# A four-layer convolution network on one core: the first layer's software pipeline regrouped into other stages, and the last layer's silu one unit later

## The chip, the cores and the metric

The kernel runs on one core of one Trainium2 chip. The metric is the device time of one execution in microseconds; before and after are compared by the medians of several runs. Engines are named as in the profile: PE is TensorE, DVE VectorE, ACT ScalarE, POOL GpSimd, SP the engine that issues most DMAs.

## The reference, cut to what matters

The input x is 8 x 16 x 128 x 128 in float32. Each of four layers adds its result on x's group norm: `x = x + layer(_gn(x))`. The edits lie in the first and the last layer.

The first layer is a small transformer block for every pixel: three tokens (columns) of 48 features (16 channels times three rows, with wrap-around), normed, attention with four heads of 12 over the tokens, a residual, a norm, an MLP of 48 to 192 to 48 with Gelu, a residual, a norm, a sum over the tokens and a 1x1 convolution:

```python
h = _ln(x)
q, k, v = jnp.split(h @ w_attn.T, 3, axis=-1)
att = softmax(einsum('nhtd,nhsd->nhts', q, k) / sqrt(12))
x = x + (att @ v) @ w_attn_proj.T
x = x + gelu(_ln(x) @ w_fc.T) @ w_fc_proj.T
x = sum(_ln(x), axis=1)          # then conv_w, conv_b
```

The last layer is a 3x3 convolution of cubic B-spline bases of x plus a 3x3 convolution of silu(x).

## The kernel before, in words

**First layer** (`layer0`). The image is cut into 64 chunks (`NCHUNKS`): two images and eight columns at a time. A token column is 128 pixels. `steps` runs 67 rounds on each engine: three lead-in rounds, a loop of three rounds a pass (`TURNS`), and the last ones written out. In round n, four chunks are in work at different stages (`STAGE`): chunk n is "new", n-1 "attn", n-2 "mlp", n-3 "out". Each engine has its own order written out in its `body`; engines meet by counting semaphores alone, so an instruction that waits holds all behind it on that engine.

- new: `centre` (3 matmuls, TensorE) removes the mean; ScalarE reads it twice (`read_centre`: Square and Copy); `var1` sums the squares with a matmul of ones, `inverse_std` takes the reciprocal root on ScalarE, `scale_tokens` multiplies on GpSimd; `heads` (10 matmuls) makes query, key and value, `read_heads` copies them; `query_key` multiplies shifted queries and keys (three on VectorE, two on GpSimd), `score` reduces, `softmax_shift` subtracts the maximum.
- attn: Exp on ScalarE, `softmax_scale`, then `values` (9 multiplications, VectorE) and `add_values` (6 additions, GpSimd), `mix` (transposes), `read_mix`, `project`, and `add_attention` (VectorE), the first residual X1.
- mlp: `square_residual` (ScalarE), `var2`, `inverse_std`, `scale_residual` (VectorE); then for six groups g of 512 pixels `hidden` (two matmuls side by side), `hidden_rest`, three Gelus on ScalarE, `shrink` back, `add_mlp` (VectorE, X2); `square_out`.
- out: `var3`, `inverse_std`, `scale_out` and `add_out` on GpSimd, and the store.

PSUM has four pairs of banks, each used as a ring: tps (centre, var1, var2, var3, mix), qps (heads), fps (hidden), cps (shrink and project). `Plan` counts the places in the rings. Before a matmul goes into a bank, its reader of two places earlier must be done. TensorE's order in a round is `centre`, `var2`, `hidden(0)`, `var1`, `var3`, then groups of `hidden`, `shrink` of the group before, `hidden_rest`, two `heads` and one `mix`, and last `project`. VectorE's: `softmax_scale`, `values(0)`, `scale_residual`, `values(1)`, `values(2)`, `add_mlp` 0 to 4, the three products, `add_mlp(5)`, and `score` alternating with `add_attention`.

**Last layer** (`layer3`). 66 units n (a chunk k of four rows, in two halves e). In each unit ScalarE makes distances and squares, VectorE cubes and bases; after each two units TensorE multiplies chunk k's bases with the spline weights (`multiply(k)`) and then does `gather(k - 2)`, which takes the silu of chunks up to k-1 and the kept planes. The silu input S is loaded by GpSimd's own DMA queue (`load_silu`, three slots): load k waits for `gather(k - 3)` and for the load before. `silu_after(n)` says after which unit ScalarE does `silu(k)`: after units 3, 5, 7 and so on. `kept_after(n)` says which planes are copied out after a unit: two on ScalarE after odd units, one after even ones.

## Time and profile before

| | us |
|---|---|
| median of three runs | 11524.5 |
| those runs, lowest to highest | 11506.01 to 11528.91 |
| the profiled execution, its own time | 11512.45 |
| its span, first to last instruction | 11510.3 |
| busy in it: PE, DVE, ACT, POOL | 8808.3, 7862.0, 7497.3, 6400.2 |
| mean granted clock of TensorE, share of full speed | 0.877 |

Busy times are of one profiled execution. Busy shares mix four layers with different limits; the first layer's loop and the last layer's are read by themselves, from the stretches in which they run.

### The profile page before, as it was taken

Reading aid. Unit: us, or ns where it says so; the run is one execution under the profiler, and the core shown is the slowest. Engines: PE = TensorE matmul, PEld = TensorE weight load, DVE = VectorE, ACT = ScalarE, POOL = GpSimd, SP = SyncE. Lnnn points to the kernel's source line nnn. Section 1 sums busy time; section 2 is a strip of 40 time slices with the busy share of each in tenths; the row PEclk is TensorE's granted clock in tenths of the full one; section 3 lists DMA queues with packets and bytes.
Section 4 is the critical chain, followed back from the end, with each engine's and each line's share of the span. In section 5 each row is a group of like instructions: output and inputs, shape, how many; then the busy total and the mean of one; then the engine's idle time right before and its main releaser. Section 6 shows DMA issues by size and latency. Waiting matters only on the chain. (4 is left out here: it accounts for less than half of the span.)

```text
span 11510.3 us, 144669 instructions
## 1 busy us (share of the span) xinstructions
PE 8808.3 (77%) x35038; PEld 2895.7 (25%) x35038; DVE 7862.0 (68%) x9543; ACT 7497.3 (65%) x8343; POOL 6400.2 (56%) x3353
## 2 busy tenths in 40 slices
PE   5888888888888888844008888888888888885588
PEld 2333323333333333311002222222222222221133
DVE  5555565555556555643748888888888888886677
ACT  3555555555555555523419889889889988985577
POOL 3444444444444444420008888888888888885111
PEclk8888888888888888877559999999999999998799
DMA  2000000000000000010432322233223322234554
GB/s 74 9 9 7 8 9 9 7 9 9 9 7 9 9 7 9 4 62 29 141 106 60 67 62 59 60 68 65 60 60 67 67 60 60 65 66 91 138 126 117
DMA packets 284359, 562.90 MB, mean 49 GB/s; under 512 B 75120, under 2 KB 205904, under 8 KB 270172
## 3 DMA queue, kind: packets, MB, share of 16 engines
q1 hardware_dynamic: 247858, 536.71, 19.5%
q0 software_dynamic: 35744, 17.87, 0.8%
q8 instruction: 259, 4.24, 0.2%
q14 instruction: 498, 4.08, 0.1%
HBM read 367.98 MB, written 186.07 MB: 48 GB/s over the span
## 5 line engine op out<-in xcount | busy, mean ns | idle before, releaser
L1188 POOL TENSOR_TENSOR l_a<-l_a 128x1018 f32<-128x1018 f32 x2116 | 3920.9, 1883 | 600.4 <-ACT l_a L1349 587.4
L1311 DVE TENSOR_TENSOR l_r<-l_pps,l_a 128x509 f32<-128x509 f32 x4232 | 2642.3, 680 | 651.7 <-PE l_pps L1201 651.6
L1349 ACT ACTIVATE l_a<-l_a 128x2036 f32<-128x2036 f32 x1193 | 2270.1, 1903 | 126.4 <-DVE l_a L1317 100.5
L1201 PE MATMUL l_qps<-l_mv,l_wst 123*128 123x509 bf16 x4246 | 1318.7, 393 | 889.0 <-DMA l_mv<-pw 567.5
L1342 ACT ACTIVATE l_a<-l_qps 128x1018 f32<-128x1018 f32 x1592 | 1591.6, 1019 | 471.9 <-PE l_qps L1201 457.1
L586 POOL TENSOR_TENSOR a_pr<-a_pr 128x768 f32<-128x768 f32 x384 | 877.1, 2284 | 1248.2 <-DVE a_pr L529 1232.4
L540 DVE TENSOR_TENSOR a_x<-a_cps,a_x 128x512 f32<-128x512 f32 x384 | 260.8, 688 | 1624.2 <-PE a_cps L417 1142.8
L665 ACT ACTIVATE a_g<-a_fps 128x512 f32<-128x512 f32 x1152 | 646.0, 595 | 1110.7 <-PE a_fps L410 848.5
L1201 PE MATMUL l_pps<-l_mv,l_wst 123*128 123x509 bf16 x4232 | 1342.9, 389 | 10.9 <-DVE l_r L1311 5.0
L1254 PE MATMUL l_aux<-l_r,l_sums 128*32 128x509 f32 x8448 | 1129.4, 607 | 54.3 <-DVE l_o L1295 33.3
L463 POOL TENSOR_TENSOR a_pr<-a_qkv 128x768 f32<-128x768 f32 x128 | 344.3, 2707 | 1256.5 <-ACT a_qkv L671 1256.5
L1317 DVE TENSOR_SCALAR l_a<-l_qps 128x1018 int32<-128x1018 int32 x796 | 961.1, 1207 | 61.6 <-PE l_qps L1201 61.6
L644 ACT ACTIVATE a_r<-a_tps,a_eps 128x512 f32<-128x512 f32 (+1 forms) x960 | 638.5, 672 | 489.0 <-PE a_tps L370 230.4
L417 PE MATMUL a_cps<-a_g,a_wfp 128*64 128x512 f32 (+1 forms) x2304 | 904.8, 680 | 0.9 <-ACT a_g L665 0.9
L1201 PEld LDWEIGHTS l_qps<-l_mv,l_wst 123*128 123x128 bf16 x4246 | 300.5, 99 | 2031.7 <-issue 1107.5
L370 PE MATMUL a_tps<-a_h,a_ones 128*128 128x512 f32 x768 | 570.2, 902 | 307.6 <-ACT a_r L644 197.8
L529 DVE TENSOR_TENSOR a_pr<-a_qkv,a_at 128x768 f32<-128x768 f32 x576 | 792.7, 1437 | 2.2
L396 PE MATMUL a_cps<-a_yt,a_wproj 96*128 96x512 f32 x768 | 551.0, 866 | 252.7 <-DVE a_x L540 238.0
L410 PE MATMUL a_fps<-a_h,a_wfc 128*128 128x512 f32 x768 | 490.0, 723 | 171.7 <-ACT a_g L665 171.7
L1201 PEld LDWEIGHTS l_pps<-l_mv,l_wst 123*128 123x128 bf16 x4232 | 420.2, 99 | 766.0 <-DVE l_r L1311 358.8
L404 PE MATMUL a_fps<-a_h,a_wfc 48*128 48x512 f32 x1536 | 493.9, 723 | 61.6 <-ACT a_g L665 48.7
L533 DVE TENSOR_TENSOR a_h<-a_x,a_r 128x512 f32<-128x512 f32 x384 | 530.9, 1446 | 4.4 <-ACT a_r L644 4.4
(178 smaller groups left out, 11989.3 us busy)
## 6 DMA issues: line engine op xcount, KB each, us to landing
l_mv<-pw SPq DMA_DIRECT2D x1608, 79.5 KB
l_gx<-g SPq DMA_DIRECT2D x66, 1040.0 KB
planes<-l_s SPq DMA_DIRECT2D x67, 1018.0 KB, 4.6
l_sh<-planes SPq DMA_DIRECT2D x536, 127.2 KB, 6.5
a_xt<-g SPq DMA_DIRECT2D x192, 160.0 KB, 3.3
pw<-pw_hi SPq DMA_DIRECT2D x165, 127.2 KB
pw<-pw_mid SPq DMA_DIRECT2D x165, 127.2 KB
pw<-pw_lo SPq DMA_DIRECT2D x165, 127.2 KB
```

The source lines that it names most:

```text
L417: last = t_.matmul(cps[lo * FS:hi * FS, c % 2, :], flat(wfp[:, m, lo:hi, :]), G[:, g % 2, m, :], start=m == 1, stop=m == 2, skip_group_che ...
L529: v.tensor_tensor(out, val, a, ALU.mult).then_inc(val_v, 1)
L586: g_.tensor_tensor(y, y, PR[:, 3 * e + d, :], ALU.add).then_inc(val_p, 1)
L644: s_.activation(r, of, ACT.Abs_reciprocal_sqrt, bias=eps[:], scale=1.0 / EMB).then_inc(t_read, 1)
L665: s_.activation(G[:, g % 2, m, :], fps[:, bank % 2, :], ACT.Gelu).then_inc(f_read, 1)
L1188: g.tensor_tensor(a, a, a, ALU.mult).then_inc(sq_p, 1)
L1201: return t.matmul(out, wst[:, k, n * P:(n + 1) * P], x[:, n // NPP, cols], start=True, stop=True)
L1254: last = t.matmul(aux[32 * pp:32 * pp + 32, 0:SUB], sums[:, 0, :], R[:, NPP * k + pp, :], start=k == 0, stop=k == NCG - 1, skip_group_chec ...
L1311: v.tensor_tensor(to, pps[:, (2 * m + h) % P_BANKS, 0:SUB], pair_of(A, m)[:, h, :], ALU.mult).then_inc(mul_done, 1)
L1317: v.tensor_scalar(pair_of(A, s).bitcast(I32), q.bitcast(I32), 0x7FFFFFFF, None, ALU.bitwise_and).then_inc(abs_v, 1)
L1342: s_.activation(pair_of(A, s), q, ACT.Abs).then_inc(abs_a, 1)
L1349: s_.activation(a, a, ACT.Abs_reciprocal_sqrt, bias=1.0).then_inc(root_done, GROUP)
```

## The change

- First layer, stages: `centre`, `var1` and `scale_tokens` are a stage "ahead" (chunk n); `heads`, the products, the scores, the softmax shift and Exp are "new" (chunk n-1); attention with `square_residual`, `var2` and `scale_residual` is "attn" (n-2); the MLP with var3, `scale_out`, `add_out` and the store is "mlp" (n-3). There are still 67 rounds, and the loop has four to a pass. Tc has four slots in place of three, the input XT two in place of three, QKV two in place of one.
- The order in each engine's `body` is new, as the diff shows. Exp stands at the end of ScalarE's round. Two `mix` each stand in groups 3, 4 and 5.
- Last layer: `silu(k)` stands after unit 2k+4 in place of 2k+3.

Index changes that only follow from the new stage numbers are left out of the diff.

```diff
-TURNS = 3
+TURNS = 4
+SLOTS0 = 2
 BANK = 512
-T_GROUPS = {"centre": (3, "new"), "var2": (6, "mlp"), "var1": (3, "new"), "var3": (6, "out"), "mix": (6, "attn")}
+T_GROUPS = {"mix": (6, "attn"), "centre": (3, "ahead"), "var1": (3, "ahead"), "var3": (6, "mlp"), "var2": (6, "attn")}
 C_GROUPS = {"mlp": (6, "mlp"), "proj": (6, "attn")}
-STAGE = {"new": 0, "attn": 1, "mlp": 2, "out": 3}
+STAGE = {"ahead": 0, "new": 1, "attn": 2, "mlp": 3}
+MIX_AT = {3: (0, 1), 4: (2, 3), 5: (4, 5)}
...
-        self.new, self.attn, self.mlp, self.out = (0 <= like - of < NCHUNKS for of in STAGE.values())
+        self.ahead, self.new, self.attn, self.mlp = (0 <= like - of < NCHUNKS for of in STAGE.values())
...
-        XT = sb("a_xt", [F2, TURNS, TW * H])
+        XT = sb("a_xt", [F2, SLOTS0, TW * H])
...
-        QKV = sb("a_qkv", [P, TW, 3 * F2])
+        QKV = sb("a_qkv", [P, 2, TW, 3 * F2])
...
-                    if n + TURNS < NCHUNKS:
+                    if n + SLOTS0 < NCHUNKS:
                         sp.wait_ge(t_made, p.t_base + p.t_at["centre"] + 3)
-                        load(n + TURNS)
-                    if p.out:
+                        load(n + SLOTS0)
+                    if p.mlp:
...
                 def heads(p, w):
                     if w == 0:
-                        pe.wait_ge(h1_made, p.n * 3 + 3)
-                    pe.wait_ge(q_read, p.n * TW + w + 1)
+                        pe.wait_ge(h1_made, p.n * 3)
+                    pe.wait_ge(q_read, (p.n - 1) * TW + w + 1)
                     t_.matmul(qps[:, w % 2, 0:3 * F2], H1[:, w * H:(w + 1) * H], wqkv[:], start=True, stop=True).then_inc(q_made, 1)
                 def mix(p, q):
                     if q % 2 == 0:
-                        pe.wait_ge(val_p, (p.n - 1) * 6 + q + 2)
+                        pe.wait_ge(val_p, (p.n - 2) * 6 + q + 2)
...
                 def body(p):
-                    if p.new:
-                        pe.wait_ge(x_in[p.turn], (p.n - p.turn) * 16 + 48)
-                        for g in range(3):
-                            centre(p, g)
-                    if p.mlp:
-                        for g in range(6):
-                            var2(p, g)
-                        hidden(p, 0)
-                    if p.new:
-                        for g in range(3):
-                            var1(p, g)
-                    if p.out:
-                        for g in range(6):
-                            var3(p, g)
                     for g in range(7):
-                        if p.mlp and 0 < g < 6:
+                        if p.mlp and g < 6:
                             hidden(p, g)
                         if p.mlp and g:
                             shrink(p, g - 1)
                         if p.mlp and g < 6:
                             hidden_rest(p, g)
-                        if p.new and 0 < g < 6:
-                            heads(p, 2 * g - 2)
-                            heads(p, 2 * g - 1)
-                        if p.attn and g:
-                            mix(p, g - 1)
+                        if p.new and g < 5:
+                            heads(p, 2 * g)
+                            heads(p, 2 * g + 1)
+                        if p.attn:
+                            for q in MIX_AT.get(g, ()):
+                                mix(p, q)
+                    if p.ahead:
+                        pe.wait_ge(x_in[p.turn % SLOTS0], (p.n - p.turn % SLOTS0) * 24 + 48)
+                    for g in range(6):
+                        if p.attn:
+                            project(p, g)
+                        if p.ahead:
+                            (centre if g < 3 else var1)(p, g % 3)
+                    if p.mlp:
+                        for g in range(6):
+                            var3(p, g)
                     if p.attn:
                         for g in range(6):
-                            project(p, g)
+                            var2(p, g)
...
-                def products(p):
-                    dve.wait_ge(q_read, p.n * TW + TW + 2)
-                    if p.attn:
-                        dve.wait_ge(val_p, p.n * 6)
-                    for d in (-1, 0, 1):
-                        query_key(v, d).then_inc(sc_v, 1)
+                def products(p, d):
+                    if d == -1:
+                        dve.wait_ge(q_read, p.n * TW + 2)
+                        if p.attn:
+                            dve.wait_ge(val_p, (p.n - 1) * 6)
+                    query_key(v, p, d).then_inc(sc_v, 1)
...
-                    if g == 0 and p.out:
+                    if g == 0:
...
                 def body(p):
                     if p.attn:
                         softmax_scale(p)
                         values(p, 0)
                     if p.mlp:
+                        add_mlp(p, 0)
+                    if p.attn:
+                        values(p, 1)
+                    if p.mlp:
+                        add_mlp(p, 1)
+                    if p.attn:
+                        values(p, 2)
+                    if p.mlp:
+                        for g in range(2, 6):
+                            add_mlp(p, g)
+                    for g in range(6):
+                        if p.attn:
+                            add_attention(p, g)
+                        if p.new and g in (1, 2, 3):
+                            products(p, g - 2)
+                    if p.new:
+                        for n in range(5):
+                            score(p, n)
+                        softmax_shift(p)
+                    if p.attn:
                         for g in range(6):
                             scale_residual(p, g)
-                    if p.attn:
-                        values(p, 1)
-                        values(p, 2)
-                    if p.mlp:
-                        for g in range(5):
-                            add_mlp(p, g)
-                    if p.new:
-                        products(p)
-                    if p.mlp:
-                        add_mlp(p, 5)
-                    for g in range(6):
-                        if p.new and g < 5:
-                            score(p, g)
-                        if p.attn:
-                            add_attention(p, g)
-                    if p.new:
-                        softmax_shift(p)
...
+                pool.sem_inc(z_made, 3)
...
                 def body(p):
                     if p.attn:
-                        add_values(p, 0)
+                        for d in range(3):
+                            add_values(p, d)
                     if p.new:
+                        pool.wait_ge(q_read, p.n * TW + 2)
+                        if p.attn:
+                            pool.wait_ge(val_p, (p.n - 1) * 6)
+                        for d in (-2, 2):
+                            query_key(g_, p, d).then_inc(sc_p, 1)
+                    if p.ahead:
                         for g in range(3):
                             scale_tokens(p, g)
-                    if p.attn:
-                        add_values(p, 1)
-                        add_values(p, 2)
-                    if p.out:
+                    if p.mlp:
                         for d in range(3):
                             scale_out(p, d)
-                    if p.new:
-                        pool.wait_ge(q_read, p.n * TW + TW + 2)
-                        if p.attn:
-                            pool.wait_ge(val_p, p.n * 6)
-                        for d in (-2, 2):
-                            query_key(g_, d).then_inc(sc_p, 1)
-                    if p.out:
                         add_out(p)
...
-                    if w == 0 and p.attn:
-                        act.wait_ge(val_v, p.n * 9)
-                    act.wait_ge(q_made, p.n * TW + w + 1)
-                    s_.activation(QKV[:, w, :], qps[:, w % 2, 0:3 * F2], ACT.Copy).then_inc(q_read, 1)
+                    act.wait_ge(q_made, (p.n - 1) * TW + w + 1)
+                    s_.activation(QKV[:, (p.turn - 1) % 2, w, :], qps[:, w % 2, 0:3 * F2], ACT.Copy).then_inc(q_read, 1)
...
                 def body(p):
-                    if p.new:
+                    for g in range(6):
+                        if p.mlp:
+                            gelu(p, g)
+                        if p.new and g < 5:
+                            read_heads(p, 2 * g)
+                            read_heads(p, 2 * g + 1)
+                        if p.attn:
+                            for q in MIX_AT.get(g, ()):
+                                read_mix(p, q)
+                        if p.mlp and g in (3, 5):
+                            square_out(p, g // 4)
+                    if p.ahead:
                         for g in range(3):
                             read_centre(p, g)
                     if p.mlp:
-                        for d in range(3):
-                            square_residual(p, d)
+                        square_out(p, 2)
+                    if p.ahead:
+                        for g, (w, n) in enumerate(CENTRE):
+                            inverse_std(p, "var1", g, R1[:, w * H:(w + n) * H])
+                    if p.mlp:
+                        act.wait_ge(stored, (p.n - 3) * (SETS * 16) + 16)
+                    for g in range(6):
+                        if p.attn and g % 2 == 0:
+                            square_residual(p, g // 2)
+                        if p.mlp:
+                            inverse_std(p, "var3", g, R3[:, g // 2, g % 2 * BANK:(g % 2 + 1) * BANK])
                     if p.attn:
-                        act.wait_ge(soft, (p.n - 1) * 9 + 6)
-                        s_.activation(At[:], At[:], ACT.Exp, scale=float(HEAD) ** -0.5).then_inc(soft_exp, 1)
-                    if p.mlp:
                         for g in range(6):
                             inverse_std(p, "var2", g, R2[:, g, :])
                     if p.new:
-                        for g, (w, n) in enumerate(CENTRE):
-                            inverse_std(p, "var1", g, R1[:, w * H:(w + n) * H])
-                    if p.out:
-                        act.wait_ge(stored, (p.n - 3) * (SETS * 16) + 16)
-                        for g in range(6):
-                            inverse_std(p, "var3", g, R3[:, g // 2, g % 2 * BANK:(g % 2 + 1) * BANK])
-                    for g in range(7):
-                        if p.mlp and g < 6:
-                            gelu(p, g)
-                        if p.new and 0 < g < 6:
-                            read_heads(p, 2 * g - 2)
-                            read_heads(p, 2 * g - 1)
-                        if p.attn and g:
-                            read_mix(p, g - 1)
-                    if p.mlp:
-                        for d in range(3):
-                            square_out(p, d)
+                        act.wait_ge(soft, (p.n - 1) * 9 + 6)
+                        s_.activation(At[:], At[:], ACT.Exp, scale=float(HEAD) ** -0.5).then_inc(soft_exp, 1)
...
             def silu_after(n):
-                return (n - 3) // PARITY if n >= 3 and n % PARITY else None
+                return (n - 4) // PARITY if n >= 4 and n % PARITY == 0 else None
```

## Rows read from the trace of the kernel before

**Rows 1.** Windows: stretch, us, busy of each engine (instructions), PEclk, DMA share, GB/s.

```profile
77.00:5063.00 4986.00, 4118.92 (x10496) 1516.03 (x10496) 2831.36 (x2816) 2570.60 (x4163) 2298.66 (x1024) 0.85 0.04 8
...
10756.00:11508.00 752.00, 649.26 (x3664) 232.80 (x3660) 552.78 (x321) 569.04 (x387) 132.71 (x190) 0.92 0.51 122
```

**Rows 2.** Timeline of TensorE, first layer: start, us, line, passes, idle before.

```profile
2504.20 2.13 PE L417 MATMUL a_cps<-a_g,a_wfp 128*128 128x512 f32 x6
...
2507.22 1.13 PE L381 MATMUL a_qps<-a_wqkv,a_h 128*128 128x288 f32 x4
2508.19 0.60 PE L389 MATMUL a_tps<-a_ident,a_pr 128*96 128x128 f32 x4
...
2509.78 2.14 PE L417 MATMUL a_cps<-a_g,a_wfp 128*128 128x512 f32 x6
...
2532.69 7.56 PE L396 MATMUL a_cps<-a_yt,a_wproj 96*128 96x512 f32 x10 [3.83 <-DVE a_x L540]
...
2569.43 2.06 PE L410 MATMUL a_fps<-a_h,a_wfc 128*128 128x512 f32 x2 [2.69 <-ACT a_g L665]
...
4983.86 1.13 PE L404 MATMUL a_fps<-a_h,a_wfc 48*128 48x512 f32 x4 [0.34 <-ACT a_g L665]
```

**Rows 3.** Windows of one round, cut at its changes of clock.

```profile
2531.83:2538.65 6.82, 5.96 (x7) 2.37 (x8) 6.82 (x10) 1.06 (x1) 4.77 (x2) 0.51 0.12 22
...
2545.48:2555.72 10.24, 7.26 (x9) 2.42 (x8) 7.01 (x7) 6.99 (x9) 2.18 (x1) 0.51 0.08 15
...
sum 77.37, PE 64.12 PEld 23.76 DVE 45.09 ACT 40.91 POOL 37.20; mean PE 9.16 PEld 3.39 DVE 6.44 ACT 5.84 POOL 5.31
```

**Rows 4.** Timeline of TensorE: `hidden(0)` of the first and last chunk, var3.

```profile
166.26 1.13 PE L404 MATMUL a_fps<-a_h,a_wfc 48*128 48x512 f32 x4 [0.75 <-DVE a_h L533]
...
5004.86 1.13 PE L404 MATMUL a_fps<-a_h,a_wfc 48*128 48x512 f32 x4
5005.92 5.85 PE L375 MATMUL a_tps<-a_sq,a_ones 128*128 128x512 f32 x12
```

**Rows 5.** Timeline of ScalarE, same round: around Exp, one Gelu.

```profile
2546.60 1.28 ACT L685 ACT_TABLE_LOAD   x1
2547.89 0.68 ACT L685 ACTIVATE a_at<-a_at 128x576 f32<-128x576 f32 x1
...
2571.52 0.60 ACT L665 ACTIVATE a_g<-a_fps 128x512 f32<-128x512 f32 x1 [1.66 <-PE a_fps L410]
```

**Rows 6.** Timeline of VectorE: values alone, then beside GpSimd's adds.

```profile
2551.63 2.69 DVE L529 TENSOR_TENSOR a_pr<-a_qkv,a_at 128x768 f32<-128x768 f32 x3
...
2562.16 10.11 DVE L529 TENSOR_TENSOR a_pr<-a_qkv,a_at 128x768 f32<-128x768 f32 x6
```

**Rows 7.** DMA issues of the page: KB each, median us to landing.

```profile
l_gx<-g SPq DMA_DIRECT2D x66, 1040.0 KB
...
a_xt<-g SPq DMA_DIRECT2D x192, 160.0 KB, 3.3
```

**Rows 8.** ScalarE's groups, 5250 to 10550 us: busy, mean ns, idle before.

```profile
L1349 ACT ACT_TABLE_LOAD x1 | 1.3, 1283 | 0.0
```

**Rows 9.** Groups of instructions, 10600 to 11511 us: the silu activations.

```profile
L1604 ACT ACTIVATE l_s<-l_s 128x1040 f32<-128x1040 f32 x33 | 35.3, 1070 | 149.4 <-DMA l_s<-g 149.4
```

**Rows 10.** ScalarE's silu(0) and silu(1), TensorE's gather(0), in order of time.

```profile
10773.73 1.07 ACT L1604 ACTIVATE l_s<-l_s 128x1040 f32<-128x1040 f32 x1
...
10791.60 1.07 ACT L1604 ACTIVATE l_s<-l_s 128x1040 f32<-128x1040 f32 x1
...
10804.29 5.33 PE L1718 MATMUL l_ops<-l_s,l_wba 128*64 128x512 f32 x36
```

**Rows 11.** GpSimd's DMA queue in order of time: a wait for the load before.

```profile
10945.63 0.66 POOL L1579 DMA_DIRECT2D l_s<-g  x1 [31.49 <-DMA l_s<-g]
```

**Rows 12.** Windows of two stretches in the last layer.

```profile
11163.00:11200.00 37.00, 37.00 (x222) 13.16 (x220) 33.44 (x20) 34.53 (x24) 8.13 (x12) 1.00 0.59 157
10924.00:10975.00 51.00, 41.17 (x236) 14.67 (x234) 33.36 (x20) 34.65 (x24) 8.52 (x12) 0.90 0.51 111
```

More of the change, by code:

```diff
@@ L166, in ring @@
         for name, (size, of) in groups.items():
-            if {"new": self.new, "attn": self.attn, "mlp": self.mlp, "out": self.out}[of]:
+            if {"ahead": self.ahead, "new": self.new, "attn": self.attn, "mlp": self.mlp}[of]:
                 at[name], k = k, k + size
@@ L283, in layer0 @@
         w_in, cw_made, cw_ready, cent_made, w_ready = (sem(f"a_{n}") for n in ("w_in", "cw_made", "cw_ready", "cent_made", "w_ready"))
-        x_in = [sem(f"a_x_in{k}") for k in range(TURNS)]
+        x_in = [sem(f"a_x_in{k}") for k in range(SLOTS0)]
         stored = sem("a_stored")
@@ L303, in load @@
                     for i in range(3):
-                        sp.dma_start(XT[i * SETS * C:(i + 1) * SETS * C, n % TURNS, :].rearrange("p (w h) -> p w h", h=H),
-                                     rows[:, w0:w0 + TW, i:i + H]).then_inc(x_in[n % TURNS], 16)
-                for n in range(TURNS):
+                        sp.dma_start(XT[i * SETS * C:(i + 1) * SETS * C, n % SLOTS0, :].rearrange("p (w h) -> p w h", h=H),
+                                     rows[:, w0:w0 + TW, i:i + H]).then_inc(x_in[n % SLOTS0], 16)
+                for n in range(SLOTS0):
                     load(n)
@@ L357, in centre @@
                     w, n = CENTRE[g]
-                    t_.matmul(place(p, "centre", g)[:, 0:n * H], flat(wcen[:]), XT[:, p.turn, w * H:(w + n) * H],
+                    t_.matmul(place(p, "centre", g)[:, 0:n * H], flat(wcen[:]), XT[:, p.turn % SLOTS0, w * H:(w + n) * H],
                               start=True, stop=True).then_inc(t_made, 1)
@@ L504, in softmax_shift @@
                 def softmax_shift(p):
-                    b = p.n * 9
-                    dve.wait_ge(sc_v, p.n * 8 + 8)
+                    b = (p.n - 1) * 9
+                    dve.wait_ge(sc_v, p.n * 8)
                     top = sm[:, 0, :].rearrange("p (d n) -> p d n", d=3)
@@ L545, in add_attention @@
                     dve.wait_ge(c_made, p.c_base + c + 1)
-                    v.tensor_tensor(X1[:, g, :], cps[:, c % 2, :], Tc[:, (p.turn - 1) % TURNS, at:at + BANK], ALU.add).then_inc(c_read, 1)
+                    v.tensor_tensor(X1[:, g, :], cps[:, c % 2, :], Tc[:, (p.turn - 2) % TURNS, at:at + BANK], ALU.add).then_inc(c_read, 1)
                 def body(p):
```

35 lines of the change are left out of this document (17 added, 18 removed).

## The prediction

> **What bounds the kernel.** I read the stages first. The first layer's loop takes 4986 us with TensorE busy 4119 of them, the last layer's loop 752 us [rows 1]; the edits touch nothing else, and the 5.7 ms between stay as they are.
>
> In the first layer I then read one round on TensorE in order of time [rows 2]. In the MLP groups the matmuls stand back to back: group to group 5.58 us, of which two `heads` 0.97. Outside them TensorE stands still: 3.83 us before `project(1)` (`add_mlp(5)` was queued behind the three products on VectorE), 2.69 us before `hidden_rest(0)` (ScalarE had var3's roots and a table load first), and others, smaller. The stages of that round show 64.12 us busy of 77.37, so 13.2 us idle, and three stretches at the granted clock 0.51, that is mostly 1.2 GHz: twice 6.8 us (the first is shown) and once 10.2; each follows such a hole [rows 3], and at 1.00 (2.4 GHz) the same work runs without loss. VectorE is busy 45, ScalarE 41, GpSimd 37 us of a round: none of them is the bound as a sum.
>
> The work of TensorE in a round at 2.4 GHz: six groups, less one pair of `heads`, 6 x 5.58 - 0.97 = 32.5; `var3`, `var2`, `project`, 12 passes of 512 columns each, 5.85 apiece [rows 4] = 17.5; `centre` and `var1`, five passes' worth each of 0.486 = 4.9. Sum 54.9. So 77.4 = 54.9 + 13.2 idle + 9.3 lost to the clock. The first chunk's `hidden` starts at 166.3 and the last one's at 5004.9 [rows 4]: 63 rounds apart, of which 61 have all four stages (rounds 3 to 63, a matter of the code).
>
> **First layer, part by part.** No arithmetic, matmul or DMA is added or removed; `centre`/`norm` of a chunk, its `heads` and products, its attention and its MLP now stand in four successive rounds, and var3 in the MLP's own. I walk the new queues from S, the end of `shrink(5)`, at full clock.
>
> TensorE has `project(g)` alternating with `centre`/`var1`, so the wait for `add_attention(g-2)` falls under the other matmul. The products stand behind `add_attention(1)`, with GpSimd's two products long done, and the only add ahead of `project(1)` is `add_mlp(5)` (0.6). Ends at S+10.7, its 10.7 of work. If the products ran at the values' shared rate, 1.69 us for 768 columns [rows 6] and so 1.9 each, `project(5)` would be some 2 us late; I take half the chance of it in the range.
>
> ScalarE is next: centre reads to S+6.1, `square_out(2)` 1.0, table load 1.3, `var1` roots to 11.2, then three squares of 1.0 among the six `var3` roots. TensorE runs two matmuls ahead of it in two banks, so `var3` and `var2` end at S+23.4 in place of 22.3: 1.1 lost. The last root ends at 24.2. Then the queue asks for a table load, Exp, a table load and Gelu: 1.28 + 0.68 + 1.28 and 0.60 [rows 5], so `hidden_rest(0)` starts at 28.2, while `hidden(0)` ended at 24.5: a hole of 3.7. The softmax shift, done at S+18.4, is no longer what Exp waits for. `scale_residual(0)` starts at 19.3, so `hidden` does not wait for it.
>
> After that 31.5 us of MLP groups: the groups without mixes have only `heads` (0.97) to cover the Gelu between `hidden_rest` and the next `hidden`; in the old tail a group with a mix alone (0.53) stood 0.34 short [rows 2], so 0.87 is enough. VectorE: scale of the softmax to 30.5 (3.0), `values(0)` to 33.1, `values(1)` and `values(2)` at the shared rate of 10.1 us for six [rows 6], to 42 and 47; `add_mlp(1)` at 42 is needed by `shrink(3)` at 47.3, the sums for `mix(0)` (39.4) at 45.5, those for `mix(4)` (49.5) at 56.7. Nothing waits: slack of 5 us and more. The x loads have two buffers in place of three, but a load of 3.3 us [rows 7] is asked for a full round ahead; the store is awaited half a round later. Both cost nothing; without that cover each would show as a wait before `centre` or before the first `var3` root.
>
> Full clock round: 54.9 + 1.1 + 3.7 = 59.7. One hole of 3.7 us is left, like the one of 3.83 after which the clock was low for 6.8 us; I charge one such stretch a round, 6.8 at half speed less what falls in the hole: 2.9. **Round 62.6.** Full rounds save 61 x (77.37 - 62.6) = 901. Fill and drain: chunk 0's Exp no longer stands before chunk 1's `var1` (first MLP at about 150, not 166), and the last MLP has no var3 of another chunk inside (5): with the lighter rounds 64 and 65, 28. Together 929.
>
> Does an interleaved Square or Copy reload a table? In layer 2 Abs, root, Square and Copy ran a whole layer on one load [rows 8]; so nothing.
>
> On `values` beside `add_values`, the row says 1.69 us each in place of 0.87. The Trainium skill, SBUF — State Buffer, "Who interferes with whom", says that a VectorE instruction with two SBUF inputs and a GpSimd one that reads SBUF block each other for whole instructions. By it every value could wait for a whole add, 2.3 us by the page of the profile, and take 3.2: `add_mlp(1)` would be 4.5 later, still inside the 5 of slack, the sum unchanged but the second last rival below nearer.
>
> **Last layer.** `silu(k)` moves one unit later in ScalarE's queue, 8.9 us (silu(0) to silu(1), two units, 17.9 [rows 10]). Its waits for the POOL queue's S load sum to 149.4 us [rows 9]. Behind it stand Squares, on which VectorE's bases and so TensorE depend. Its user, `gather(k-1)`, starts 11.7 us after it (silu(1) ends 10792.7, gather(0) starts 10804.3) [rows 10], so 2 us of slack remain and the move itself costs nothing. If loads came as they do, each wait would shrink by up to 8.9: 105 of the 149. But the POOL queue waited up to 31.5 us for a load to land [rows 11], beside gx loads of 1040 KB a unit [rows 7], and when ScalarE no longer stops, gx loads no longer pause. A stretch without stalls moved 157 GB/s with TensorE always busy, one with them 111 [rows 12]: the room is there at times only. Bounds 0 and 105; I take 45, nearer the zero since the load's own length stays. The Trainium skill, SBUF — State Buffer, "SBUF: two separate sides", says that descriptors for a DMA of the GpSimd queue can't be written while VectorE is in a two-port operation. By that the loads lengthen as VectorE's pauses vanish, and this part would be worth 0.
>
> **Sum.** 11512.5 (the profiled execution; span 11510.3 and 2.1 around it) - 929 - 45 = 10538, say 10540. The runs shown have a median of 11524.5, 12 more; a tenth of a per cent, left aside. No change can be told within 0.2%, some 23 us.
>
> **Rivals.**
> - Forecast, a round of 61 to 65 us: 0.60. With the last layer's bounds 10,380 to 10,730.
> - The clock never falls in the 3.7 us hole: round 59.7, 61 x 2.9 = 177 less: 10,360. The holes of 2.69 and 3.83 speak against. 0.10.
> - The clock stays low longer, or falls again between var3's roots where TensorE waits 0.3 to 0.5 each time; before it once stayed for 10.2 us [rows 3]. 3.4 us more a round: 10,750. With late products, 10,870. 0.19.
> - ScalarE reloads tables after all, six loads of 1.28 in the stretch it sets: 7.7 a round, 11,010. The single load of [rows 8] speaks against. 0.04.
> - The other side: the values under the MLP hold `add_mlp(1)`, `shrink(3)` waits, and the six values before it decide. From 5 us late each microsecond costs one a round; from 20 us late, when they take 4.5 us each and not 1.3, the change is slower. At 5.5 each: 25 late, round 82.7, 11,512 + 61 x 5.3 - 45 = 11,790. Nothing in [rows 6] shows such rates. 0.03.
> - The old bound was not TensorE's queue but something I have not seen, and the round stays near 77: 11,470 to 11,530. Against: the gaps close exactly where the trace names them. 0.04, half of it within 0.2%.
>
> **Numbers.** The range takes the first three, with some of the clock's bad side: 10,350 to 10,850 leaves out under 0.2. Faster: all but the last two, with half of the last lying below: 0.95; same 0.02, slower 0.03.
>
> **What would show it.** Right: rounds of 61 to 65 us, four to a loop pass, TensorE busy some 58 of them; one hole of 3 to 4 us before `hidden_rest(0)` put down to Gelu, no hole before `project(1)`; one stretch of low clock a round and the mean clock of the layer above 0.93; no wait of `mix` for GpSimd; Silu's waits below 105 us and no new wait of `gather` over 4 us. Wrong: a wait of `shrink` for `add_mlp`, more than three table loads a round, two low stretches, or silu waits of the same sum as before.

## The result, and the profile after

| us | before | after |
|---|---|---|
| median | 11518.51 (4 runs) | 10461.89 (4 runs) |
| lowest to highest | 11506.01 to 11528.91 | 10454.87 to 10472.31 |
| span of the profiled execution | 11510.3 | 10453.1 |
| mean granted clock | 0.877 | 0.912 |

The ratio is 0.9084, 95% interval 0.9068 to 0.9100: 1057 us less, where 10540 with a range of 10350 to 10850 was predicted. The windows of the two stages of the kernel after correspond to [rows 1]:

```profile
77.00:4060.00 3983.00, 3662.69 (x10494) 1439.99 (x10492) 2709.98 (x2816) 2516.70 (x4162) 2046.02 (x1024) 0.94 0.05 11
9755.00:10451.00 696.00, 612.69 (x3624) 223.22 (x3620) 544.07 (x316) 556.29 (x382) 122.28 (x184) 0.94 0.54 130
```

The same work now fills 92% of the first layer's loop (83% before) at a granted clock of 0.94 (0.85 before). The first layer can be accounted for by TensorE's `hidden(0)`; those of its first and last chunk correspond to [rows 4], and between them stands the one of chunk 61, with which the last full round ends:

```profile
149.83 1.13 PE L406 MATMUL a_fps<-a_h,a_wfc 48*128 48x512 f32 x4 [0.38 <-DVE a_h L531]
...
3897.74 1.69 PE L406 MATMUL a_fps<-a_h,a_wfc 48*128 48x512 f32 x4 [3.09 <-DVE a_h L531]
...
4008.98 1.13 PE L406 MATMUL a_fps<-a_h,a_wfc 48*128 48x512 f32 x4
```

In the kernel before, chunk 61's is this one:

```profile
4877.89 1.13 PE L404 MATMUL a_fps<-a_h,a_wfc 48*128 48x512 f32 x4
```

The 63 rounds from the first to the last took 4838.60 us before and 3859.15 now, 979.4 less. The 61 full rounds among them took 4711.6 before and 3747.9 now, that is 77.24 and 61.44 each, 963.7 less; the two lighter ones behind them give 15.7. The first `hidden(0)` is 16.4 earlier. The layer's end, read at the next layer's first DMA, went from 5064.15 to 4061.46, so it follows the last `hidden(0)` by 52.5 in place of 59.3: 6.8 more. Together 1002.7. The spans differ by 1057.2, which leaves 54.5 for everything behind the first layer, the silu's move in it.

One round of TensorE in order of time corresponds to [rows 2]; S, the end of `shrink(5)` of the round before, is at 2520.36, and the next S at 2583.28:

```profile
2520.36 1.13 PE L398 MATMUL a_cps<-a_yt,a_wproj 96*128 96x512 f32 x2
2521.32 1.02 PE L360 MATMUL a_tps<-a_xt,a_wcen 96*128 96x512 f32 x2
...
2529.92 1.94 PE L377 MATMUL a_tps<-a_sq,a_ones 128*128 128x512 f32 x4
2532.26 4.08 PE L377 MATMUL a_tps<-a_sq,a_ones 128*128 128x512 f32 x8 [0.40 <-ACT a_r L643]
2536.64 5.97 PE L372 MATMUL a_tps<-a_h,a_ones 128*128 128x512 f32 x12 [0.29 <-ACT a_r L643]
2545.43 1.13 PE L406 MATMUL a_fps<-a_h,a_wfc 48*128 48x512 f32 x4 [2.82 <-DVE a_h L531]
2547.29 2.08 PE L412 MATMUL a_fps<-a_h,a_wfc 128*128 128x512 f32 x2 [0.73 <-ACT a_g L664]
...
2553.23 3.81 PE L419 MATMUL a_cps<-a_g,a_wfp 128*128 128x512 f32 x6
```

The idle times are 0.40, 0.29, 2.82 and 0.73: 4.2 of 62.9. The holes of 3.83 and 2.69 are gone; what is left is one pair of holes around `hidden(0)`, the larger one not before `hidden_rest(0)` but before `hidden(0)` itself, put down to VectorE's `scale_residual`. Windows cut around it, and one at the same place of the round before, show the clock: it is the number behind the five busy times.

```profile
2485.10:2491.90 6.80, 6.13 (x12) 2.36 (x10) 6.70 (x10) 2.77 (x6) 0.03 (x1) 0.50 0.02 4
...
2520.36:2545.43 25.07, 21.39 (x50) 8.35 (x49) 22.35 (x23) 19.39 (x29) 15.00 (x8) 1.00 0.09 21
...
2547.80:2555.50 7.70, 7.70 (x14) 2.62 (x14) 6.02 (x7) 2.50 (x5) 2.37 (x1) 0.50 0.00 0
2555.50:2581.60 26.10, 26.10 (x95) 10.75 (x94) 9.63 (x11) 13.69 (x28) 14.03 (x8) 0.98 0.00 1
```

One stretch at 0.50 (1.2 GHz) follows the hole. In the round shown it is 10.2 us long (2546.5 to 2556.8), in the round before 6.8, and 6.8 is the rule: of the 61 full rounds six take 62.9 us or more, like the one shown, most others 61.3. That is the forecast stretch. Why `hidden(0)` waits is in VectorE's rows, and why nothing could have started earlier anyway in ScalarE's, which correspond to [rows 5]. VectorE:

```profile
2535.51 2.16 DVE L510 TENSOR_TENSOR a_at<-a_sc,a_sm 128x192 f32<-128x192 f32 x1
2537.70 0.37 DVE L509 TENSOR_REDUCE a_sm<-a_sc 128x64 f32<-128x192 f32 x1
2538.11 1.99 DVE L510 TENSOR_TENSOR a_at<-a_sc,a_sm 128x192 f32<-128x192 f32 x1
...
2542.68 2.60 DVE L531 TENSOR_TENSOR a_h<-a_x,a_r 128x512 f32<-128x512 f32 x1 [0.15 <-DVE a_at L510]
```

GpSimd at the same time, and then ScalarE:

```profile
2532.77 7.12 POOL L598 TENSOR_TENSOR a_r<-a_x,a_r 128x1024 f32<-128x1024 f32 x3 [0.51 <-ACT a_r L643]
```

```profile
2543.35 1.28 ACT L705 ACT_TABLE_LOAD   x1
2544.65 0.68 ACT L705 ACTIVATE a_at<-a_at 128x576 f32<-128x576 f32 x1
2545.35 1.28 ACT L664 ACT_TABLE_LOAD   x1
2546.64 1.08 ACT L664 ACTIVATE a_g<-a_fps 128x512 f32<-128x512 f32 x2
```

A subtraction of 192 elements a partition takes 2 us while GpSimd multiplies beside it (the third one, 2.00, runs beside GpSimd's addition of `add_out`); the reductions between, which read one tile, keep their 0.37. The shift therefore ends at S+22.2, not S+18.4, and `scale_residual(0)` starts 3 us late. Then it takes 2.60 us itself, beside GpSimd's second addition of 2.34, where the six of the round together take 5.61. ScalarE is not free for Gelu before 2546.64 in any case.

In the last layer the group of silus (the second row) corresponds to [rows 9]; the first row is `gather`'s silu part, which waits for it:

```profile
L1717 PE MATMUL l_ops<-l_s,l_wba 128*64 128x256 f32 (+1 forms) x1152 | 188.7, 483 | 68.9 <-ACT l_s L1603 68.9
...
L1603 ACT ACTIVATE l_s<-l_s 128x1040 f32<-128x1040 f32 x33 | 35.1, 1064 | 97.5 <-DMA l_s<-g 97.4
```

Silu's waits fell from 149.4 to 97.5 us, and `gather`'s waits for silu rose from 17.8 to 68.9, up to 11.5 at once. TensorE's wait for the bases went from 121.1 to 88.4 and that for the kept planes from 37.9 to 0.

### The profile page after: what moved, and what is told of

Its sections match the earlier page's. It is cut to its first block and busy times, and to the rows that moved or that the text cites. A ratio compares the mean times of both kernels' runs of the same rounds, so it can differ in the third digit from the quotient of the medians.

```text
span 10453.1 us, 144566 instructions
## 1 busy us (share of the span) xinstructions
PE 8327.9 (80%) x35038; PEld 2814.5 (27%) x35038; DVE 7741.3 (74%) x9543; ACT 7442.2 (71%) x8342; POOL 6142.6 (59%) x3353
## 5 line engine op out<-in xcount | busy, mean ns | idle before, releaser
L588 POOL TENSOR_TENSOR a_pr<-a_pr 128x768 f32<-128x768 f32 x384 | 854.0, 2224 | 739.3 <-DVE a_pr L527 723.4
L419 PE MATMUL a_cps<-a_g,a_wfp 128*64 128x512 f32 (+1 forms) x2304 | 832.1, 635 | 0.7 <-ACT a_g L664 0.7
L527 DVE TENSOR_TENSOR a_pr<-a_qkv,a_at 128x768 f32<-128x768 f32 x576 | 714.9, 1294 | 2.2
L594 POOL TENSOR_TENSOR a_h<-a_tc,a_r 128x512 f32<-128x512 f32 (+1 forms) x192 | 205.2, 1097 | 845.0 <-ACT a_r L643 845.0
L598 POOL TENSOR_TENSOR a_r<-a_x,a_r 128x1024 f32<-128x1024 f32 x192 | 454.7, 2399 | 98.4 <-ACT a_r L643 98.4
L1578 POOL DMA_DIRECT2D l_s<-g x66 | 44.6, 676 | 687.0 <-DMA l_s<-g 388.3
L383 PE MATMUL a_qps<-a_wqkv,a_h 128*128 128x288 f32 x1280 | 429.3, 465 | 9.6 <-POOL a_h L594 6.8
```

Source lines behind the costliest of these rows:

```text
L419: last = t_.matmul(cps[lo * FS:hi * FS, c % 2, :], flat(wfp[:, m, lo:hi, :]), G[:, g % 2, m, :], start=m == 1, stop=m == 2, skip_group_che ...
L527: v.tensor_tensor(out, val, a, ALU.mult).then_inc(val_v, 1)
L588: g_.tensor_tensor(y, y, PR[:, 3 * e + d, :], ALU.add).then_inc(val_p, 1)
```

## Experiments

Each kernel differs from the one after the change by the edit shown, unless it says otherwise; ratios are to the kernel before, with 95% intervals.

### The two parts by themselves

The first kernel is the one after with the old `silu_after`; the second is the one before with the new `silu_after`:

```diff
-                return (n - 4) // PARITY if n >= 4 and n % PARITY == 0 else None
+                return (n - 3) // PARITY if n >= 3 and n % PARITY else None
```

> The changed kernel with the last layer's silu put back after unit 2k+3. My theory (the two parts add up, the silu's part is worth about 50 us): 10,510 us, silu waits back near 149 us. Rival (the last layer is bound by its DMA traffic and the silu's place is worth nothing, the 54 us were shift between layers): 10,462 within 15 us.

Measured: 10511.41, ratio 0.9121 (0.9105 to 0.9136). Silu waited 159.4 us.

> The kernel before with the silu alone moved to unit 2k+4. Additive: 11,465 us, ratio 0.9955, and in the trace the waits move in part from ScalarE's Silu to TensorE's gather, sum of Silu waits near 98 us. Rival (DMA bound): ratio 1.000 within 0.002.

Measured: 11481.12, ratio 0.9962 (0.9946 to 0.9978). Silu waited 102.9 us, `gather` for it 72.8.

The silu's move is worth 36 us alone and 50 on top of the first layer's change (43 by the two ratios): the parts add up within the intervals. The first layer's change alone gives 1006, near the 1002.7 of its account above.

### Is it the alternation, or only the stages?

```diff
-                    for g in range(6):
-                        if p.attn:
+                    if p.attn:
+                        for g in range(6):
                             project(p, g)
-                        if p.ahead:
-                            (centre if g < 3 else var1)(p, g % 3)
+                    if p.ahead:
+                        for g in range(3):
+                            centre(p, g)
+                        for g in range(3):
+                            var1(p, g)
```

> The changed kernel with the six project matmuls first, then the centre and var1 ones, instead of one of each in turn. In the trace of the changed kernel a 512-column matmul in turn took 0.86 us, and 0.97 where a matmul follows one of the same bank ring. My theory: 0.97 is the round trip of two banks (matmul, its reader, the next matmul), so without the turns the stretch grows by 11 x 0.11 = 1.2 us plus waits for the products between the adds, 2 to 4 us a round, 10,590 to 10,700. Rival (0.86 comes from something else, such as the size of the operands): start to start stays 0.86 and the time grows only by the products' waits, under 60 us.

Measured: 10673.0, ratio 0.9263 (0.9248 to 0.9279), 211 us above the kernel after, 3.5 a round. TensorE's timeline shows where they go:

```profile
2537.03 1.12 PE L398 MATMUL a_cps<-a_yt,a_wproj 96*128 96x512 f32 x2 [0.44 <-DVE a_x L547]
2538.69 1.12 PE L398 MATMUL a_cps<-a_yt,a_wproj 96*128 96x512 f32 x2 [0.54 <-DVE a_x L547]
2541.85 0.70 PE L360 MATMUL a_tps<-a_xt,a_wcen 96*128 96x256 f32 x2 [0.32 <-ACT a_tc L652]
2542.93 1.98 PE L367 MATMUL a_tps<-a_sq,a_ones 128*128 128x512 f32 x4 [0.38 <-ACT a_tc L652]
2546.42 0.69 PE L367 MATMUL a_tps<-a_sq,a_ones 128*128 128x256 f32 x2 [1.51 <-ACT a_r L646]
2546.99 1.98 PE L377 MATMUL a_tps<-a_sq,a_ones 128*128 128x512 f32 x4
```

These are the waits for the reader of a bank, with no other matmul under them. From S (2532.69 here) to the first `var3` matmul it is 14.3 us, where the kernel after needs 9.6: 4.7 more. That the round grows by 3.5 only goes with the clock, whose mean over 500 to 3800 us is 0.97 here and 0.94 in the kernel after. And the four undisturbed `project` matmuls of this kernel start every 0.95 to 0.96 us (3.90 for the four, as 5.85 for six in [rows 4]), where those of the kernel after start every 0.86. The next kernel asks which of the two is the matmul's own time: on top of the edit above, `project(2)` and `project(3)` go into the heads' banks, and `add_attention` reads them there, so that a bank's reader has longer.

```diff
-                    pe.wait_ge(c_read, p.c_base + c + 1)
-                    t_.matmul(cps[:, c % 2, :], flat(wproj[:]), yT[:, g, :], start=True, stop=True).then_inc(c_made, 1)
+                    if g in (2, 3):
+                        pe.wait_ge(q_read, min(p.n, NCHUNKS) * TW + 2 if isinstance(p.n, int) else p.n * TW + 2)
+                        to = qps[:, g % 2, :]
+                    elif g >= 4:
+                        pe.wait_ge(c_read, p.c_base + c - 1)
+                        to = cps[:, c % 2, :]
...
+                    t_.matmul(to, flat(wproj[:]), yT[:, g, :], start=True, stop=True).then_inc(c_made, 1)
```

> Like the run without the turns, but project(2) and project(3) write the two banks that the heads use, so no project waits for the add two before it until project(4). Round-trip theory: start to start of the projects falls to 0.86 at least for the first four. Rival (matmuls with the same weights one after the other take 0.97 whatever the bank): 0.97 stays.

Measured: 10624.58, ratio 0.9227 (0.9212 to 0.9243), 48 less than with two banks. Pairs of `project`, TensorE's timeline:

```profile
2564.77 1.88 PE L406 MATMUL a_qps<-a_yt,a_wproj 96*128 96x512 f32 x4
2566.49 1.88 PE L406 MATMUL a_cps<-a_yt,a_wproj 96*128 96x512 f32 x4
2568.21 1.88 PE L360 MATMUL a_tps<-a_xt,a_wcen 96*128 96x512 f32 x4
...
2575.55 1.98 PE L377 MATMUL a_tps<-a_sq,a_ones 128*128 128x512 f32 x4
```

1.72 from pair to pair, 0.86 a matmul: the 0.97 that I had read as a matmul's duration is the round trip of a ring of two banks, that is matmul, reader, next matmul into the same bank. From S (2562.95) to `var3` it is now 12.6 us, 1.7 less than with two banks, and the round 0.8 less, at a mean clock of 0.95. The waits of `centre` and `var1` stayed (0.32, 0.38, 1.51), so more banks for `project` alone don't replace the alternation.

### What is behind the hole that is left

The rows suggest two chains that end together: VectorE's and ScalarE's. The first kernel shortens ScalarE's chain by one table load: Square stands in for Exp, so the attention weights are other numbers.

```diff
-                        s_.activation(At[:], At[:], ACT.Exp, scale=float(HEAD) ** -0.5).then_inc(soft_exp, 1)
+                        s_.activation(At[:], At[:], ACT.Square, scale=float(HEAD) ** -0.5).then_inc(soft_exp, 1)
```

> The changed kernel with Square in place of Exp in the softmax (the attention weights are then others, all else is computed as before), so that ScalarE has one table load less, 1.28 us, between the last root and the first Gelu. My theory: two chains end together at hidden_rest(0), ScalarE's (Exp and its loads) and VectorE's (the shift's three subtractions, 2.0 us each beside GpSimd's multiplications and not 0.36, then scale_residual(0), for which hidden(0) waits 2.8 us). Then this gains at most 0.1 us a round: 10,455 to 10,470. Rival (ScalarE's chain alone sets it, as predicted): 1.28 x 63 = 80 us less, 10,380.

Measured: 10470.94, ratio 0.9093 (0.9079 to 0.9107): no gain. `hidden(0)` waits 2.80 for `scale_residual` as before. The second kernel takes GpSimd's multiplications, and the additions behind them, away from the shift:

```diff
                     if p.mlp:
+                        if p.new:
+                            pool.wait_ge(soft, (p.n - 1) * 9 + 6)
                         for d in range(3):
                             scale_out(p, d)
```

> The changed kernel with GpSimd's scale_out held until the softmax shift of the round is done. The shift's subtractions should take 0.36 us each again, and hidden(0) should no longer wait for scale_residual(0). My theory of two chains that end together: the time stays, 10,440 to 10,480, since ScalarE's chain still sets the first Gelu, and the hole moves to hidden_rest(0). Rival (the block on VectorE alone costs the hole): 2.8 x 63 = 176 us less, 10,290.

Measured: 10459.74, ratio 0.9080 (0.9067 to 0.9092): no gain either, but the rows move. VectorE's shift, then TensorE:

```profile
2537.95 0.36 DVE L510 TENSOR_TENSOR a_at<-a_sc,a_sm 128x192 f32<-128x192 f32 x1
2538.34 0.37 DVE L509 TENSOR_REDUCE a_sm<-a_sc 128x64 f32<-128x192 f32 x1
2538.75 0.36 DVE L510 TENSOR_TENSOR a_at<-a_sc,a_sm 128x192 f32<-128x192 f32 x1
```

```profile
2544.98 1.13 PE L406 MATMUL a_fps<-a_h,a_wfc 48*128 48x512 f32 x4
2549.73 1.12 PE L412 MATMUL a_fps<-a_h,a_wfc 128*128 128x512 f32 x2 [3.62 <-ACT a_g L666]
```

That is the round the prediction had walked: no wait of `hidden(0)`, one hole of 3.6 before `hidden_rest(0)`. The subtraction takes 0.36 us alone and 2.0 beside GpSimd's multiplications. Now both edits in one kernel:

> The after kernel with Square in place of Exp (the attention weights are other numbers) and GpSimd's scale_out held until the softmax shift is done. Each of the two alone left the time as it was. Theory (two chains end within half a microsecond of each other before hidden(0) and hidden_rest(0): VectorE's shift and scale_residual, ScalarE's two table loads and Gelu): with both shortened the hole shrinks by the one table load, 1.28 us a round, 61 x 1.28 = 78 us: about 10,380, with one hole of 2.3 us before hidden_rest(0). If that shorter hole no longer brings the granted clock down, another 61 x 2 us: about 10,260. Rival (a third thing sets the hole, neither chain): 10,460 again.

Measured: 10304.96, ratio 0.8952 (0.8931 to 0.8973): 157 us less than the kernel after, where neither edit alone moved anything. It is more than the 78 of the table load, and less than with a clock that never falls; over 500 to 3800 us the mean clock is 0.97, with either edit alone 0.94. Windows that begin at the end of the hole (at 2503.7 after one of 2.96, at the others after one of 2.20) show the clock:

```profile
2503.70:2512.00 8.30, 7.59 (x15) 3.02 (x16) 8.27 (x6) 4.08 (x7) 5.34 (x2) 0.59 0.11 20
2565.40:2573.00 7.60, 7.57 (x18) 3.14 (x19) 7.57 (x6) 2.97 (x6) 5.10 (x2) 0.79 0.10 17
2623.90:2632.00 8.10, 8.03 (x26) 3.21 (x26) 8.06 (x6) 4.21 (x10) 5.15 (x2) 1.00 0.10 16
```

After the holes of 2.20 the granted clock stays at 1.00 in one round and falls for a part of the stretch in others; the hole of 2.96 comes once in four rounds and is put down to no other engine:

```profile
PE a_fps L412 <- ACT a_g L666: 105.5, 57, 2.2
PE a_fps L406 <- issue: 37.9, 13, 3.3
```

From 500 to 3800 us there are thirteen such waits, 2.9 each, always before the first matmul of a loop pass of four rounds: that is the place of the way back to the loop's start. In the kernel after, the hole before `hidden(0)` is as long as they are, so they don't show there and come out when it closes.

### What the clock itself costs

Four matmuls whose result nobody reads stand before `hidden(0)`, in the bank that it overwrites:

```diff
                 def body(p):
+                    if p.mlp:
+                        pe.wait_ge(f_read, (p.n - 3) * 18 + 2)
+                        for _ in range(FILL):
+                            t_.matmul(fps[:, 0, 0:3 * P], ones[:], wfp[:].rearrange("p m s f -> p (m s f)"), start=True, stop=True)
                     for g in range(7):
```

> The changed kernel with four extra matmuls of 384 columns on constant weights, about 0.64 us each, into the hidden banks in the hole before hidden(0); their results are overwritten. Theory (the low clock after the hole is what it costs, 2.9 us a round): granted clock of the layer near 1.00 and 10,290 to 10,350. Rival (the clock falls anyway, or the extra work comes late and pushes hidden(0)): 10,460 to 10,520.

Measured: 10316.84, ratio 0.8956 (0.8943 to 0.8968), 145 us less than the kernel after, with no wait taken away but the filled one. From 500 to 3800 us the granted clock is 1.00 with the extra work, 0.94 without. Two extra matmuls in place of four, and four with the GpSimd edit from above:

> Two extra matmuls before hidden(0) in place of four: 1.95 us of the 2.8 us hole before hidden(0) is filled, 0.9 us stays open, and the 0.7 us before hidden_rest(0) too. Theory A (any hole under some 2 us is ridden out: the holes of 0.3 to 0.7 us that the round has elsewhere did not bring the clock down): granted clock near 1.00, 10,310 to 10,330. Theory B (it takes a nearly closed hole): the clock falls in part of the rounds, mean 0.94 to 0.98 in the first layer, 10,360 to 10,460.

> Four extra matmuls before hidden(0), as in the kernel with the filled hole (10,317 us), and GpSimd's scale_out held until the softmax shift is done. Theory (the gain of the filled hole is the clock's alone): hidden(0) never waits for scale_residual, the extra matmuls end 0.2 us later than ScalarE's chain needs, the clock stays at 1.00 and the time is that of the filled hole, 10,300 to 10,330. Rival: with both chains off VectorE's shift, hidden_rest(0) starts up to 0.5 us earlier a round: 10,290. A result above 10,400 would say that what was left of the hole lay behind the extra matmuls and brings the clock down again.

Measured: two matmuls 10332.25, ratio 0.8980 (0.8965 to 0.8995); four with GpSimd behind the shift 10322.03, ratio 0.8969 (0.8954 to 0.8984). The two-matmul kernel still has a hole before `hidden(0)`, on TensorE's timeline:

```profile
2581.98 1.13 PE L407 MATMUL a_fps<-a_h,a_wfc 48*128 48x512 f32 x4 [1.53 <-DVE a_h L536]
2583.85 1.13 PE L413 MATMUL a_fps<-a_h,a_wfc 128*128 128x512 f32 x2 [0.74 <-ACT a_g L669]
```

and its granted clock is 0.99 over 500 to 3800 us. The first window below begins at that `hidden(0)`. The other two begin at the extra matmuls behind the hole at the loop's start, in two passes that follow each other: the hole was 3.05 us in the one and 3.09 in the other.

```profile
2581.00:2592.00 11.00, 9.28 (x30) 3.52 (x30) 10.90 (x14) 6.94 (x13) 2.59 (x2) 1.00 0.07 12
2517.97:2526.00 8.03, 7.35 (x12) 2.92 (x13) 7.93 (x11) 2.67 (x4) 0.57 (x1) 0.50 0.08 16
...
2282.73:2291.00 8.27, 7.59 (x24) 2.83 (x24) 8.10 (x11) 4.76 (x8) 0.86 (x1) 1.00 0.08 15
```

After 3.05 the granted clock is 0.50, after 3.09 it stays at 1.00. From 500 to 3800 us, windows of some 8 us show it at 1.00 after 38 of this kernel's 43 holes of about 1.5 us before `hidden(0)`, and below (0.57 to 0.79) after the other five. It stays at 1.00 after four of this kernel's thirteen holes at the loop's start (2.5 to 3.1 us), and after eight of the thirteen (2.5 to 3.05) in the kernel with four extra matmuls; after the others it falls for all or a part of the stretch. So in these two kernels the length of the hole alone does not decide it.

What the extra matmuls bring back is the clock's part, 130 to 145 us; the two chains behind the hole stay, and moving GpSimd adds nothing that the intervals show. The three filled kernels can't be told apart by their intervals; each beats both the kernel before and the one after. The 10304.96 of the kernel with both shortened chains does not stand beside them, since Square is not the reference's Exp.

### The last layer: who paces silu

One more unit of delay:

```diff
-                return (n - 4) // PARITY if n >= 4 and n % PARITY == 0 else None
+                return (n - 5) // PARITY if n >= 5 and n % PARITY else None
```

> The after kernel with silu(k) after unit 2k+5 in place of 2k+4 in the last layer. Theory (after the first move gather already waits for silu 69 us in all, up to 9.5 at once, so what ScalarE no longer waits TensorE does): silu's own waits fall from 97 to 40 to 60 us, gather's rise by more than as much, to 150 us or over, and the time is 0 to 60 us longer: 10,460 to 10,520. Rival (ScalarE's waits are what the layer pays, TensorE has 83 us idle in it to give): another 20 to 45 us less, 10,415 to 10,440.

Measured: 10474.5, ratio 0.9096 (0.9081 to 0.9112), not told from the kernel after. Its two groups:

```profile
L1717 PE MATMUL l_ops<-l_s,l_wba 128*64 128x256 f32 (+1 forms) x1152 | 195.0, 495 | 87.3 <-ACT l_s L1603 87.3
...
L1603 ACT ACTIVATE l_s<-l_s 128x1040 f32<-128x1040 f32 x33 | 35.2, 1068 | 100.0 <-DMA l_s<-g 99.9
```

The time lies in the range of the theory, and the rival's further gain did not come; but silu's waits did not fall to 40 to 60 us, and `gather`'s rose to 87 and not to 150. The waits of silu for its load and of `gather` for silu together were 167 us before, 166 after and 187 here: the first move shifted them to an engine that had them to give, the second adds to `gather`'s alone. A reading that fits, and that no run isolates: the load of S waits for `gather(k - 3)` in its turn and comes later with it (GpSimd's queue waited 116.8 us for `gather` after the change, up to 25.8 at once, and 123.4 here, up to 41.9). Then the load itself, from GpSimd's queue to SP's (`load_silu` moves with its calls):

```diff
+                    if n == 2:
+                        for i in range(PSLOTS):
+                            load_silu(i)
+                    elif n % PARITY and (n - 5) // PARITY >= PSLOTS:
+                        load_silu((n - 5) // PARITY)
                     if n >= GX:
                         sp.wait_ge(v_done, n - GX + 1)
...
-                for k in range(NCK):
-                    load_silu(k)
```

> The changed kernel with the last layer's S loads on SP's queue, among the gx loads, in place of GpSimd's. Rival A (the loads are late because GpSimd writes their descriptors beside VectorE): loads land in some 15 us, silu and gather waits go, 10,350 to 10,400. Rival B (the DMA traffic sets it: S and gx loads share the engines): the waits stay or move to the gx loads, 10,440 to 10,520. I hold B the likelier.

Measured: 10685.44, ratio 0.9271 (0.9257 to 0.9285), 224 us slower than the kernel after. Its waits:

```profile
ACT l_vb L1598 <- DMA l_gx<-g: 394.0, 31, 50.9
...
PE l_ops L1719 <- ACT l_s L1605: 211.3, 28, 9.1
```

Silu waits 4.9 us for its load now, but ScalarE waits 394 for gx, 66 before this edit: the waits of the S loads stand ahead of the gx loads in one queue (SP waits 247.8 us there for the S load before). The waits moved to the gx loads, as rival B has it, but by the order of one queue, which tells nothing of shared DMA engines, and the time is 165 us above its range. So this kernel doesn't tell what makes a load of GpSimd's queue late, and neither expectation is borne out.

## Why the prediction was right, by its own steps

- **The sum.** 929 + 45 = 974 forecast, 1057 measured. The first layer gave 1002.7 (74 more), the rest 54.5 (9 more).
- **Round 62.6.** The full rounds take 61.44 on average, where 77.24 was their average before (77.37 was one round), and save 963.7 where 901 was forecast, 63 more; a fill and drain 11 larger than forecast (below) makes it 74. The forecast had S to `hidden_rest(0)` 28.2 and from there 31.5 + 2.9; the rows show 26.9, and in the round before the one shown, with its low stretch of 6.8 us, 34.3 (2486.07 to 2520.36). The kernel with four extra matmuls, whose clock stays up, needs 31.5 for the same work (2524.72 to 2556.19). So the MLP's part and the clock's 2.9 are both right to 0.1.
- **The mis-sized term: 5.85 for 12 passes of `project`, 10.7 us for it with `centre` and `var1`.** It took 9.6. The 0.97 a matmul of [rows 4] holds the round trip of two banks; where another ring's matmul lies between, it is 0.86, and the four-bank kernel shows the same without alternation. This is the term that made the round shorter than forecast. ScalarE's last root ends at S+23.0, not 24.2, and everything behind it is earlier by that.
- **Softmax shift done at S+18.4, `hidden(0)` not waiting.** Wrong: S+22.2, and `hidden(0)` waits 2.8. I had weighed the Trainium skill's rule in SBUF — State Buffer, "Who interferes with whom", for the values and not for the small subtractions; there the trace agrees with it, 0.36 alone and 2.0 beside GpSimd. It cost nothing, since ScalarE's table loads end at the same time: removing either alone gives 0, both 157. That the time did not suffer from this step is luck: the prediction counted on ScalarE's chain alone. It is why `hidden(0)`, and not `hidden_rest(0)`, has the larger hole.
- **One hole of 3.7, after it a clock stretch of 2.9.** Right in size: 2.82 + 0.73, and filling it gives 145 us, 2.4 a round of 61; the once-in-four hole at the loop's start stays in that kernel.
- **No reload by interleaved Square or Copy.** Right: three loads a round, one each before var1's roots, Exp and Gelu; none at the squares or copies between the roots.
- **Values under the MLP cost nothing.** Right: neither `mix` nor `shrink` has a wait among the layer's. The six were priced at 10.1 us; they take 2.68 and 3.66, since GpSimd's adds run between them for the most part.
- **Fill and drain, 28.** Of the measured 1002.7 the full rounds leave 39: the first `hidden(0)` 16.4 earlier, as forecast, the two lighter rounds 15.7 and the end 6.8.
- **Silu 45, bounds 0 and 105.** 36 alone, 43 to 55 on top. "No new wait of `gather` over 4 us" was wrong: up to 11.5. The slack of 2 us was read from one silu that had not waited; a late load takes it whole. TensorE gained in two other places, its wait for the bases (121.1 to 88.4) and for the kept planes (37.9 to 0). By the Trainium skill's SBUF — State Buffer, "SBUF: two separate sides", as the prediction applied it, this part would have been 0. The gain of 36 to 55 is against that as a full account, but no run here isolates it, and whether VectorE's operations in this layer are two-port ones was not looked into.

The range's lower end held versions that the experiments reached: 10,360 with a clock that never falls was priced 177 below the forecast; measured, it is 145 below the result. That rival was wrong for this change, whose clock fell in every round, and near to what the clock is worth to the next one.

**Open:** why some S loads of GpSimd's queue take some 30 us (its queue waited 388 us in all, 19 times, up to 35, for the load before). A fourth slot for S was not tried, and a queue of its own for it neither.

## What to carry to other kernels

Before you take a matmul's spacing for its cost, look at the ring: two banks with a reader of another engine set a spacing of their own (0.96 here), and a matmul of another ring between hides it (0.86). When an edit that shortens the named wait gains nothing, shorten what ends just behind it too, in one kernel: here 0 and 0 made 157. The hole of 2.8 + 0.7 us cost itself and what the clock did after it. Where such a hole can't be closed, matmuls whose result nobody reads can bring the second part back: here 130 us of 10,460 with two of them, 145 with four.

## What the hardware showed that I had not expected

- A VectorE subtraction of 128 x 192 elements took 2.0 us beside GpSimd's multiplications of 128 x 1024 and 0.36 alone. A VectorE reduction of one tile took 0.37 in both cases.
- TensorE's granted clock stayed at 1.00 over 38 of 43 pairs of holes of about 1.5 + 0.7 us, stayed or fell for a part of the stretch after holes of 2.20, and fell after the pair of 2.82 + 0.73 in every round from 500 to 3800 us of the kernel after. After the holes of 2.5 to 3.1 us that stood once in four rounds before the extra matmuls it fell in some loop passes and stayed at 1.00 in others: 0.50 after 3.05, 1.00 after 3.09, in one kernel.
- TensorE stood for 2.5 to 3.3 us at the start of a loop pass, once in four rounds, with nothing that it waited for; the other three rounds of a pass had no such wait. That it is the jump back is read from its place; no run isolates it.
